# Two residual graph layers on one core: initial loads reordered and merged, weights split one at a time between the first steps

## The reference

```
# layer 0: attention with 12 heads of 32 features
q, k, v = x @ Wq + bq, x @ Wk + bk, x @ Wv + bv
scores = q @ k.T / sqrt(32) + beta * adj      # per head; -9e15 where adj <= 0
h = layernorm(x + softmax(scores) @ v)
# layer 1: an inner layer, run twice (l = 0, 1)
a = softmax(h @ h.T / sqrt(384)) * adj;  a = a / (sum(a) + 1e-10)
ctx = upper(a) @ (h @ Wl.T + bl) + diag(a) * (h @ Ws.T + bs) + lower(a) @ (h @ Wr.T + br)
h' = relu(layernorm(ctx) * g + b)
out = layernorm(h + h')
```

## Time and profile before

| what | value |
|---|---|
| times of three runs | 1422.78, 1424.4, 1428.75 us; median 1424.4 |
| the profiled execution | 1425.35 us, of it 1423.6 us span |
| busy: TensorE / VectorE / ScalarE / GpSimd | 1350.1 / 1078.4 / 743.9 / 610.3 us |
| share of the span | 95% / 76% / 52% / 43% |
| instructions | 37486 |
| DMA | 62.74 MB, mean 44 GB/s; 238 GB/s in the first of 40 slices |
| chain that ended last | TensorE 74%, issue 9%, GpSimd 6%, ScalarE 4%, VectorE 4%, DMA 1% |

### The profile page before, as it was taken

One profiled execution on the slowest core, in us unless ns is written; L12 is line 12 of the kernel. 1 busy time (PEld: TensorE's weight loads), 2 busy tenths in 40 slices (PEclk: granted clock), 3 DMA queues, 4 the chain that ended last, 5 costly groups with the idle time before them and its releaser, 6 DMA issues.

```text
span 1423.6 us, 37486 instructions
## 1 busy us (share of the span) xinstructions
PE 1350.1 (95%) x13568; PEld 1318.4 (93%) x13568; DVE 1078.4 (76%) x2665; ACT 743.9 (52%) x1579; POOL 610.3 (43%) x656
## 2 busy tenths in 40 slices
PE   3799999999999999999999999999999999999984
PEld 3799999999999999999999999999999999999984
DVE  3358777787887787877787877778888778777766
ACT  3355555555554555554555555555555455554553
POOL 1344444444444444444444444444344444434342
PEclk8899999999999999999999999999999999999997
DMA  7210011111011111011111011111101111101000
GB/s 238 74 39 23 29 50 50 50 49 32 16 48 48 48 48 48 5 44 48 48 48 48 18 30 48 48 48 48 31 17 48 48 48 48 48 2 39 24 13 23
DMA packets 49445, 62.74 MB, mean 44 GB/s; under 512 B 14320, under 2 KB 35952, under 8 KB 49392
## 3 DMA queue, kind: packets, MB, share of 16 engines
q1 hardware_dynamic: 49392, 62.03, 14.2%
HBM read 36.44 MB, written 12.58 MB: 34 GB/s over the span
## 4 chain that ended last, share of the span: by engine, by line
PE 74%; issue 9%; POOL 6%; ACT 4%; DVE 4%; DMA 1%; ACTq 0%; SPq 0%; POOLq 0%; DVEq 0%
PE bank L315 20%; PE bank L316 19%; PE bank L317 19%; PE bank L392 4%; PE bank L378 3%; POOL hlr_lo L995 3%; PE bank L426 3%; PE bank L364 3%; POOL h L1003 2%; PE bank L413 2%; PE bank L403 2%; DMA late<-in_w 1%; ACT hlr_hi L595 1%; POOL ln_rstd L1008 1%; ACT h L614 1%
## 5 line engine op out<-in xcount | busy, mean ns | idle before, releaser
L315 PE MATMUL bank<-w_hi,hT_hi 128*128 128x384 f32 x1152 | 402.2, 349 | 1.4 <-issue 0.9
L316 PE MATMUL bank<-w_lo,hT_hi 128*128 128x384 f32 x1152 | 389.9, 338 | 0.0
L317 PE MATMUL bank<-w_hi,hT_lo 128*128 128x384 f32 x1152 | 389.5, 338 | 0.0
L995 POOL TENSOR_TENSOR hlr_lo<-late,hlr_hi 128x384 fp32r<-128x384 f32 x256 | 253.7, 1001 | 315.5 <-ACT hlr_hi L595 314.8
L315 PEld LDWEIGHTS bank<-w_hi,hT_hi 128*128 128x128 f32 x1152 | 216.3, 188 | 6.1 <-issue 1.6
L316 PEld LDWEIGHTS bank<-w_lo,hT_hi 128*128 128x128 f32 x1152 | 216.7, 188 | 0.0
L317 PEld LDWEIGHTS bank<-w_hi,hT_lo 128*128 128x128 f32 x1152 | 216.3, 188 | 0.0
L796 DVE TENSOR_TENSOR late<-bank,rows 128x384 f32<-128x384 f32 x256 | 142.1, 555 | 87.6 <-PE bank L317 86.9
L595 ACT ACTIVATE hlr_hi<-late 128x384 fp32r<-128x384 f32 x256 | 130.5, 521 | 145.5 <-DVE late L796 141.3
L1008 POOL TENSOR_TENSOR ln_rstd<-ln_var,minus_half 128x2 f32<-128x2 f32 x128 | 98.7, 771 | 225.4 <-DVE ln_var L865 117.5
L315 PE MATMUL bank<-xT_hi,w_hi 128*128 128x256 f32 x576 | 164.6, 286 | 9.0 <-ACT kT L534 9.0
(11 more groups left out here) (93 smaller groups left out, 2876.2 us busy)
## 6 DMA issues: line engine op xcount, KB each, us to landing
v_halves<-v_stage SPq DMA_DIRECT2D x128, 99.0 KB, 2.3
xT_in<-in_xT SPq DMA_DIRECT2D x32, 384.0 KB, 3.1
x_in<-in_x SPq DMA_DIRECT2D x32, 384.0 KB, 3.8
out<-late SPq DMA_DIRECT2D x32, 384.0 KB, 2.4
late<-in_w SPq DMA_DIRECT2D x9, 576.0 KB, 5.8
adj_in<-in_adj SPq DMA_DIRECT2D x32, 64.0 KB, 3.5
adjT_in<-in_adjT SPq DMA_DIRECT2D x64, 32.0 KB, 2.8
rows<-in_bl SPq DMA_DIRECT2D x2, 192.0 KB, 6.4
```

What stands on the lines that cost most here:

```text
L315: nc.tensor.matmul(o, l_hi, r_hi, start=n == 0, stop=False)
L316: nc.tensor.matmul(o, l_hi, r_lo, start=False, stop=False)
L317: done = nc.tensor.matmul(o, l_lo, r_hi, start=False, stop=n == last)
L995: nc.gpsimd.tensor_tensor(hlr_lo[:, t, m, 0:D], hlr[:, t, m], hlr_hi[:, t, m, 0:D].bitcast(F32), ALU.subtract).then_inc(hlrlo_ready, 1)
```

## The change

It touches the first two steps only (and what they load).

- **Loads.** The four column vectors come from one array, in one DMA into one tile `columns`; eight of the nine row vectors come in one DMA (3072 values to each partition); bv stays by itself. The new order of issue: xT of unit 0, weight 0, columns, beta, weights 1 and 2, bv; in step -2 weights 3, 4, 5, xT of unit 1, x and adj of unit 0, the row vectors, then the moves of V; in step -1 weights 6, 7, 8 ahead of the loads of the next units.
- **Splits.** xT_hi comes first on ScalarE. Weight 0 is split in three pieces (kc 0, 1, 2) with semaphores of their own (`wv_hi_set`, `wv_lo_set`), and TensorE waits for them piece by piece. Then bq is scaled. Weights 1, 2 and 3 are split ahead of the first Q and K, weight 4 between takes 0 and 1, weight 5 behind take 2; 6, 7 and 8 in step -1, behind the second exp, behind take 1 and behind take 2. On VectorE the low parts of 4 and 5 stand behind `stage_v` and ahead of `make_add`, 6 ahead of `stage_v` of unit 1, 7 behind it, 8 between `stats_outer` and `shift`.
- **Waits.** `stage_v` waits for bv alone, the first bias of the inner layer for the row vectors.

```
-            sp.dma_start(bq_col[:, :], bq).then_inc(cols_in, 16)
...
+            sp.dma_start(columns[:, :, :], cols).then_inc(cols_in, 16)
             sp.dma_start(beta_col[:, :], beta.partition_broadcast(P)).then_inc(cols_in, 16)
-            for n in range(1, RAW):
-                raw_weight(n)
-            for at, vector in enumerate([bv, bl[0], br[0], bs[0], bl[1], br[1], bs[1], g1, b1]):
-                sp.dma_start(rows[:, at, :], vector.partition_broadcast(P)).then_inc(consts_in, 16)
+            raw_weight(1)
+            raw_weight(2)
+            sp.dma_start(bv_row, bv.partition_broadcast(P)).then_inc(bv_in, 16)
...
             def step(st):
                 if st.fixed and st.unit(EARLY) == 0:
-                    for n in range(RAW, NW):
+                    for n in (3, 4, 5):
+                        raw_weight(n)
+                if st.fixed and st.unit(MID) == 0:
+                    for n in (6, 7, 8):
                         raw_weight(n)
...
+                if st.fixed and st.unit(EARLY) == 0:
+                    sp.dma_start(rows[:, 1:9, :].rearrange("p r d -> p (r d)"), vectors.partition_broadcast(P)
+                                 ).then_inc(rows_in, 16)
...
-                    product(V_BANKS[t][:, 0:D],
-                            [((xT_hi[:, kc, tok], xT_lo[:, kc, tok]), weight(W_V, kc)) for kc in range(KC)]
-                            ).then_inc(v_psum, 1)
+                    for kc in range(KC):
+                        if st.fixed and st.unit(EARLY) == 0 and t == 0:
+                            pe.wait_ge(wv_hi_set, kc + 1)
+                            pe.wait_ge(wv_lo_set, kc + 1)
+                        done = product(V_BANKS[t][:, 0:D], [((xT_hi[:, kc, tok], xT_lo[:, kc, tok]), weight(W_V, kc))],
+                                       first=kc == 0, final=kc == KC - 1)
+                    done.then_inc(v_psum, 1)
...
-            act.wait_ge(cols_in, 80)
-            nc.scalar.mul(bq_col[:, :], bq_col[:, :], SCALE_ATT).then_inc(bq_scaled, 1)
-            act.wait_ge(bq_scaled, 1)
+            def split_v_weight():
+                act.wait_ge(raw_in[W_V], 16)
+                for kc in range(KC):
+                    nc.scalar.activation(w_hi[:, W_V, kc], w_raw[W_V][:, kc], ACT.Copy).then_inc(wv_hi_set, 1)
...
-                    dve.wait_ge(consts_in, 9 * 16)
+                    dve.wait_ge(bv_in, 16)
```

More of the change, by code:

```diff
@@ L310, in _, with product @@
         def _(pe):
-            def product(o, pairs):
+            def product(o, pairs, first=True, final=True):
                 last = len(pairs) - 1
                 for n, ((l_hi, l_lo), (r_hi, r_lo)) in enumerate(pairs):
-                    nc.tensor.matmul(o, l_hi, r_hi, start=n == 0, stop=False)
+                    nc.tensor.matmul(o, l_hi, r_hi, start=first and n == 0, stop=False)
                     nc.tensor.matmul(o, l_hi, r_lo, start=False, stop=False)
-                    done = nc.tensor.matmul(o, l_lo, r_hi, start=False, stop=n == last)
+                    done = nc.tensor.matmul(o, l_lo, r_hi, start=False, stop=final and n == last)
                 return done
@@ L325, in project_v @@
                 need(pe, xlo_ready, st.count(EARLY, 1, 1))
-                if st.fixed and st.unit(EARLY) == 0:
-                    pe.wait_ge(w_hi_set, 1)
-                    pe.wait_ge(w_lo_set, 1)
                 need(pe, s_masked, st.count(MID, 4, 4))
@@ L528, in take_qk @@
             def take_qk(st, m):
+                if st.fixed and st.unit(EARLY) == 0 and m == 0:
+                    act.wait_ge(bq_scaled, 1)
                 need(act, qk_psum, st.count(EARLY, 3, m + 1))
@@ L621, in normalize_inner @@
                                          scale=ln1_rstd[:, t:t + 1]).then_inc(z_ready, 1)
-            split_weight(0)
-            split_weight(1)
-            split_weight(2)
             def step(st):
                 late, mid, early, final = st.has(LATE), st.has(MID), st.has(EARLY), st.has(FINAL)
+                begin = st.fixed and st.unit(EARLY) == 0
+                second = st.fixed and st.unit(MID) == 0
                 if early:
                     split_x(st)
+                if begin:
+                    split_v_weight()
+                    scale_bq()
+                    split_weight(1)
+                    split_weight(2)
+                    split_weight(3)
                 if late:
                     take_hT(st)
-                if st.fixed and st.unit(EARLY) == 0:
-                    for n in range(3, NW):
-                        split_weight(n)
-                if late:
                     exp_gram(st, 0)
@@ L647, in step @@
                     exp_scores(st, 1)
+                if second:
+                    split_weight(6)
                 if early:
                     take_qk(st, 0)
+                if begin:
+                    split_weight(4)
+                if early:
                     take_qk(st, 1)
+                if second:
+                    split_weight(7)
                 if late:
@@ L658, in step @@
                     take_qk(st, 2)
+                if begin:
+                    split_weight(5)
+                if second:
+                    split_weight(8)
                 if late:
@@ L793, in sides_bias @@
                 k = 2 * t + m + 1
+                if st.fixed and st.unit(LATE) == 0 and l == 0 and k == 1:
+                    dve.wait_ge(rows_in, 16)
                 need(dve, hlr_psum, st.count(LATE, 8, 4 * l + k))
```

59 lines of the change are left out of this document (37 added, 22 removed).

## The result

The changed kernel took 1430.03 us (median of 17 runs, 1425.82 to 1433.57), the kernel before 1425.71 beside it (17 runs, 1422.18 to 1429.33): ratio 1.003, 95% interval 1.0021 to 1.004. The forecast was 1412.0, the range ended at 1416.4. So the time went the other way, by 4.3 us where 13 were to be won. The profiled execution of the changed kernel has a span of 1426.1 us, 2.5 more than before.

A forecast was written before the change was run, and what follows sets the result against it. TensorE bounds the kernel from 62 us on; before, a chain of its waits does. The profiled 1425.35 less 12.9 won by h's transposes is 1412.4, 1411.5 against the median; forecast 1412, range 1408.3 to 1416.4.

The forecast's parts named there:

- Behind 62 us the order is the old one: After the h transposes: nothing changes, so the 12.9 us won by then stay won to the end.
- Rival D: Behind 62 us: the gain is given back, say by loads meeting other work; 1418 to 1425 us, chance 0.04.
- V of unit 0: TensorE's first matmuls: start at 6.9 instead of 15.15 us, 8.2 won, with weight 0 split in pieces.
- The exclusion that the prediction used for unit 1: Before V of unit 1: GpSimd's xT_lo and VectorE's mask wait for one another; xT_lo goes first, ending at 25.4 us.
- Weight 2: Ahead of Q/K of unit 0: it comes between 9.3 and 10.7 us, taken as 10.2, so Q/K starts at 12.8.
- Part 2 and scores: Unit 0: Q/K part 2 starts at 18.0 us, 15.1 won; scores at 21.2, 17.0 won, with the clock up.
- V of unit 1: After unit 0's masked scores: starts at 28.0 instead of 42.13 us, 14.1 won, the mask waiting for xT_lo.
- rival A: Nothing excludes anything: mask ahead of xT_lo, split 8 costs 0.5, V of unit 1 at 26.3; 1410.0 us, chance 0.33.
- Transposes of probs: After V of unit 1: 8.9 us later, at 36.9, at half clock; h's transposes follow at 48.8, 12.9 won.
- Split 8: Its low part between ln_var and ln_shift on VectorE, beside GpSimd's ln_rstd: costs 0.5 or 1.2 us, taken as 1.2.
- Rivals B and C: B: weights 3 and 4 land late, 1416.4 us, 0.08. C: row vectors' load blocks weights 6 to 8, some 1438, 0.03.

The follow-up runs named there:

- the changed kernel with the order fixed: The changed kernel, with GpSimd waiting for VectorE's aT_lo before the last hlr_lo of the second inner layer; 1415.48 us, ratio 0.9924.
- the addresses put back: The changed kernel plus one unused 64-byte tile behind beta_col, so ident and all later tiles have their old addresses; 1415.03 us, ratio 0.9919.
- the kernel with all repairs: The changed kernel plus 64 unused bytes, GpSimd's last hlr_lo behind aT_lo, beta's load behind bv's, unit 0's mask and score_add before split 5, split 8's low part behind ln_shift; 1411.8 us.
- the kernel with the moved addresses and the fixed order: The kernel before, with four column vectors in one tile (later tiles 64 bytes lower) and GpSimd's last hlr_lo behind VectorE's aT_lo; 1426.56 us, ratio 0.9997.
- the inner layers back: The changed kernel plus an unused 64-byte tile ahead of hT, so the inner layers' tiles have their old addresses; 1420.13 us, ratio 0.9963.

## Why the prediction was wrong

**The step that failed** is the last sentence of the sum, "Behind 62 us the order is the old one", with the premise under it: "an earlier arrival at 61.71 moves the rest of the program as a whole", since TensorE is busy 57.82 of 58 us there. The order of the instructions is the old one. But TensorE's 0.54 to 0.69 us of waiting in each step hang on a tie between VectorE and GpSimd that comes out in VectorE's favour in every step of the profiled execution before. The tie costs 0.72 us when it is lost, and with the merged column tile it was lost in 18 of 24 steps: 13 us over the loop. Rival D named this place (the gain given back behind 62 us) and gave it 0.04, with loads that meet other work as the cause; the cause is another, and the loss, 13.0, lies just beyond what D allowed. The forecast, the 1.9 that the beginning won less, and 13.0 make 1426.9; the profiled execution took 1427.88. The median run took 2.2 more still; more lost steps would explain it, but no such run was profiled. The share of busy TensorE argued against it in the prediction: it says how little is won by removing the waits, not how much is lost when a wait grows.

What remains, with the loss taken away: the changed kernel with the order fixed took 0.9924 of before, 10.8 us less; with the addresses put back 0.9919. Both are 1415 us and lie inside the range. Term by term:

- **V of unit 0, 6.9 forecast, 7.28 measured.** xT_lo ended at 6.71, inside 6.4 to 6.8. The low parts of weight 0 were ready to start at 5.87, but took 2.19 us for the three pieces beside it (1.50 in the kernel with all repairs, where they start behind xT_lo), so piece 0 was late. The exclusion that the prediction used for unit 1 holds here too, and was left out. V itself took 5.8 us and not the old 4.51: 15 of its 18 matmuls came 0.32 us behind the one ahead, where 7 did before. The prediction says that the first ones ran at half clock before; the granted clock in the profile is 1.00 there, before as in the changed kernel, so it doesn't bear this out. Neither error cost anything, since Q/K waited 1.24 us more for weight 2.
- **Weight 2, copied from 11.60 and not 10.2.** This is the largest missed term of the beginning, and it put Q/K at 14.30 instead of 12.8. In the five executions of this load order it was 10.84 to 12.50, never inside the bounds of 9.3 and 10.7. The issues did come earlier, as reckoned (weight 1 at 2.67 instead of 4.09), but weight 1 then took 6.7 to 8.4 us to land, where it had taken 5.2; the prediction let the landing time stay as it was. Beta isn't what weight 1 waited for, though it came late too (at 8.8, 6.6 us after its issue, instead of at 7.3): ScalarE had scaled bq by 9.05 and then stood 1.20 us for weight 1 itself. ScalarE in the changed kernel:

```profile
8.85 0.20 ACT L527 ACTIVATE columns<-columns 128x3 f32<-128x3 f32 x1 [2.25 <-DMA beta_col<-in_beta]
10.24 1.16 ACT L531 ACTIVATE w_hi<-late 128x1152 fp32r<-128x1152 f32 x1 [1.20 <-DMA late<-in_w]
11.60 1.16 ACT L531 ACTIVATE w_hi<-late 128x1152 fp32r<-128x1152 f32 x1 [0.19 <-DMA late<-in_w]
```

By the Trainium skill (DMA: Bandwidth & Descriptors, section Anatomy of one DMA) a DMA has some 2 us of fixed cost; an estimate from that is that three loads fewer would have been worth up to 6 us if these costs ran one after the other. The section describes DMAs that GpSimd issues, and these are issued by SyncE; no run here shows any such gain.
- **Part 2 and scores.** 5.6 and 3.3 us against 5.2 and 3.2: the clock stayed up, and the copies hid splits 3 and 4 as reckoned. Of the extra 0.4 about half is in the matmuls of parts 0 and 1 (4.6 us instead of 4.4) and the rest in TensorE's wait for kT, 1.02 where 0.75 was taken. Split 4 isn't in it: ScalarE was through with it and idle for 0.20 us before take 1.
- **V of unit 1, the mechanism confirmed.** 6.8 us from scores, 6.8 forecast. The mask takes 1.82 us beside xT_lo, where it took 0.22; rival A (a mask of 0.22) falls. VectorE, then GpSimd, of the changed kernel:

```profile
24.25 1.36 DVE L713 TENSOR_TENSOR w_lo<-late,w_hi 128x1152 fp32r<-128x1152 f32 x1 [4.16 <-ACT w_hi L531]
25.52 1.82 DVE L749 TENSOR_SCALAR score_mask<-adj_in 128x128 f32<-128x128 f32 x1
27.38 0.44 DVE L752 SCALAR_TENSOR_TENSOR score_add<-adj_in,beta_col,score_mask 128x128 f32<-128x128 f32 x1
27.93 1.95 DVE L762 TENSOR_TENSOR probs<-bank,score_add 128x384 f32<-128x384 f32 x4
...
47.81 1.36 DVE L713 TENSOR_TENSOR w_lo<-late,w_hi 128x1152 fp32r<-128x1152 f32 x1
49.77 0.16 DVE L728 SCALAR_TENSOR_TENSOR ln_shift<-ln_mv,ln_rstd 128x2 f32<-128x2 f32 x1 [0.60 <-POOL ln_rstd L1051]
```

```profile
25.02 2.24 POOL L1008 TENSOR_TENSOR xT_lo<-xT_in,xT_hi 128x768 fp32r<-128x768 f32 x1 [18.31 <-ACT xT_hi L538]
...
47.98 1.75 POOL L1051 TENSOR_TENSOR ln_rstd<-ln_var,minus_half 128x2 f32<-128x2 f32 x1 [1.09 <-DVE ln_var L786]
```

- **Transposes of probs, 8.93 against 8.9**, and of h, 11.8 against 11.9. Split 8 (47.81) meets ln_rstd (47.98), which takes 1.75 instead of 0.70; the wait grew by 1.04, near the 1.2 that was taken and far from the 0.5.
- **Rivals B and C.** TensorE waited for none of the weights 3 to 8. The one load of row vectors landed 9.1 us after its issue, with no one waiting.

So the beginning won 11.0 instead of 12.9; of the missing 1.9 weight 2 is 1.5 and part 2 0.4. The loop then took 13.0 back.

## What to carry to other kernels

Before trusting a steady state that the change doesn't touch, look in it for operations of VectorE and GpSimd that start within some tens of nanoseconds of each other with TensorE waiting for one of them: write their order down with a semaphore, which here cost nothing (ratio 0.9997) and gave the old pace of the loop at both placements at which it was tried. A change that merges or drops tiles moves all tiles behind them; compare with an unused tile in their place before blaming the change itself. And 1 us at the beginning is below what four runs or one trace can tell: with the same beginning, Q/K started anywhere from 13.54 to 15.21 in five traces, because the loads landed at other times. Judge such a change by the waits that repeat from trace to trace (5.55 to 3.15 us here), and read several executions before giving a load's arrival a cause.

## What the runs showed of the hardware

- A move of tiles by 64 bytes changed the mean duration of matmuls of the same shape: in the loop, w_hi with hT_hi between 346 and 349 ns, xT_hi with w_hi between 284 and 287. A step has 108 matmuls of w with hT and 54 of xT with w. With all later tiles 64 bytes lower (the kernel with the moved addresses and the fixed order) TensorE's wait for aT_lo grew by 0.16 us a step and the step stayed as it was; at two other placements it was longer (42.43 and 42.35 instead of 42.28 on average). By which mechanism, no run tells.
- Two requests for the port 7 to 13 ns apart in the trace came out one way in 24 of 24 steps in seven kernels, and the other way in 18 of 24 in one. One of the seven has its tiles where that one has them, so a placement doesn't settle the outcome alone. That the outcome also varies from run to run fits the spread (1425.8 to 1433.6 over 17 runs of the changed kernel; 1413.9 to 1415.3 over 4 with the addresses back), but only one execution of each was profiled, so this is argued and not shown.
- TensorE's granted clock was 0.92 in the stretch with the wait of 2.53 us and 0.50 (1.2 GHz) behind it, though TensorE had worked for 4.9 us ahead; the prediction had only the fall of the earlier trace rows, 4.2 us into a wait, to go by. With the inner layers back a wait of 2.54 us was followed by 0.64 (14.9 to 19.0). A wait of 2.14 us with the order fixed, and those of 1.24 and 1.02 us in the changed kernel, left it at 1.00.
- A load's time to land depended on when it was issued and differed between executions of one order. Beta's 0.5 KB, in front of two weights of 576 KB, took 5.7 to 7.5 us in the five executions with the new beginning (issued at 2.19) and 3.4 to 5.0 in the six with the old one (issued at 3.61). Weight 0, issued at 1.3 in all thirteen, took 3.9 to 5.9.
- The first step behind the loop takes 43.9 to 45.4 us where its neighbours take 42.2 to 42.4, in every kernel (45.1 before, 43.9 changed, 45.4 with all repairs), with TensorE waiting 1.7 to 3.2 us in these three. So 1 to 2 us won at the beginning can be gone at the end, and no run here says why.
